# A stage of eight experts: dense tiles of tokens, and most tiles turned by DMA instead of by TensorE

## What is computed

```python
g = flat @ shared_gate.T
u = flat @ shared_up.T
shared_out = jax.nn.sigmoid(g) * u @ shared_down.T
weights = jax.nn.softmax(flat @ router_w.T, axis=-1)
top_w, top_idx = jax.lax.top_k(weights, TOPK)
comb = jnp.zeros_like(weights).at[jnp.arange(N)[:, None], top_idx].add(top_w)
ge = jnp.einsum('nh,eih->nei', xb, wg)
ue = jnp.einsum('nh,eih->nei', xb, wu)
he = jax.nn.sigmoid(ge) * ue
de = jnp.einsum('nei,ehi->neh', he, wd)
routed = (comb.astype(jnp.bfloat16)[:, :, None] * de).astype(jnp.float32).sum(axis=1)
return x + shared_out + routed
```

## Time and profile before

| what | value |
|---|---|
| time, median of 3 executions | 659.87 us (655.4 to 660.19) |
| the profiled execution | 653.7 us, of which its span is 651.7 us |
| granted TensorE clock over the span | 0.995 |
| busy share of the span | PE 93%, DVE 78%, ACT 72%, POOL 55% |
| busy tenths per fortieth of the span, from 80% to 95% of it (most of the expert stage) | PE 9, DVE 4 or 5, ACT 5 to 7 |

### The profile page before, as it was taken

One profiled execution on the slowest core, in us unless ns is written; L12 is line 12 of the kernel. 1 busy time (PEld: TensorE's weight loads), 2 busy tenths in 40 slices (PEclk: granted clock), 3 DMA queues, 4 the chain that ended last, 5 costly groups with the idle time before them and its releaser, 6 DMA issues.

```text
span 651.7 us, 12576 instructions
## 1 busy us (share of the span) xinstructions
PE 606.6 (93%) x4110; PEld 259.2 (40%) x4110; DVE 507.6 (78%) x970; ACT 472.0 (72%) x662; POOL 360.0 (55%) x494
## 2 busy tenths in 40 slices
PE   4799999999999999999999999879999999999987
PEld 4543333333333333333333332224554466666532
DVE  2479899999999999999999999964528654454577
ACT  3654899899899899899898888985432276667511
POOL 5559453684684684684684462251553577777310
PEclk9899999999999999999999999999999999999999
DMA  8642434534525535534433432115698533333178
GB/s 293 195 135 76 114 93 145 168 110 144 170 87 168 167 89 171 167 112 146 135 111 102 132 111 80 50 52 121 170 220 184 110 105 106 100 106 107 50 230 310
DMA packets 64990, 88.66 MB, mean 136 GB/s; under 512 B 12624, under 2 KB 45264, under 8 KB 63904
## 3 DMA queue, kind: packets, MB, share of 16 engines
q1 hardware_dynamic: 60032, 68.72, 34.4%
q0 software_dynamic: 4896, 19.14, 12.1%
HBM read 63.75 MB, written 32.74 MB: 148 GB/s over the span
## 4 chain that ended last, share of the span: by engine, by line
PE 76%; DVE 11%; issue 6%; ACT 5%; DMA 1%; POOL 1%; SPq 0%; ACTq 0%; DVEq 0%; POOLq 0%
PE PS L1083 17%; PE PS L986 11%; PE PS L1311 9%; PE PS L1055 8%; PE PS L1774 7%; DVE MX L996 7%; PE PS L845 5%; PE PS L1837 4%; PE PS L1585 4%; ACT E L1069 2%; PE PS L840 2%; PE PS L991 1%; PE PS L933 1%; PE PS L1732 1%; PE PS L929 1%
## 5 line engine op out<-in xcount | busy, mean ns | idle before, releaser
L996 DVE TENSOR_REDUCE MX<-PS 128x1 f32<-128x512 f32 x512 | 323.1, 683 | 17.3 <-PE PS L986 15.4
L1069 ACT ACTIVATE E<-PS 128x1024 f32<-128x1024 f32 x256 | 253.5, 1020 | 32.7 <-PE PS L1055 28.6
L986 PE MATMUL PS<-BIG 53*128 53x512 f16 x512 | 128.6, 384 | 12.2 <-DVE MX L996 10.8
L1083 PE MATMUL PS<-E,BIG 128*32 128x512 f32 x1024 | 136.4, 605 | 2.0 <-ACT E L1069 2.0
L1055 PE MATMUL PS<-BIG 55*128 55x512 f16 x512 | 101.2, 381 | 8.2 <-ACT E L1069 3.5
L879 POOL TENSOR_TENSOR ML<-BIG,ML 128x512 f32<-128x512 f32 x30 | 38.3, 1277 | 102.8 <-ACT BIG L855 102.6
L986 PEld LDWEIGHTS PS<-BIG 53*128 53x128 f16 x512 | 34.3, 93 | 134.0 <-DVE MX L996 120.1
L1796 DVE SCALAR_TENSOR_TENSOR E<-WP,PS 128x352 bf16<-128x352 f32 x39 | 20.3, 521 | 47.0 <-ACT WP L1786 47.0
L1774 PE MATMUL PS<-BIG,CT 128*128 x312 | 53.0, 313 | 1.8 <-DVE WP L1346 1.0
L855 ACT ACTIVATE BIG<-PS,BIG 128x256 f32<-128x256 f32 x64 | 35.7, 560 | 25.9 <-PE PS L840 14.5
L1856 POOL DMA_INDIRECT scr_ys<-SW,bvB x39 | 38.3, 981 | 20.8 <-DVE SW L1849 12.5
(11 more groups left out here) (261 smaller groups left out, 904.0 us busy)
## 6 DMA issues: line engine op xcount, KB each, us to landing
scr_parts<-WP SPq DMA_DIRECT2D x96, 128.0 KB
BIG<-scr_parts SPq DMA_DIRECT2D x64, 192.0 KB
BIG<-in_we POOLq DMA_DIRECT2D x8, 1088.0 KB, 14.1
scr_u<-ML SPq DMA_DIRECT2D x32, 256.0 KB, 3.0
X<-in_x SPq DMA_DIRECT2D x8, 512.0 KB, 6.5
CT<-in_ctx SPq DMA_DIRECT2D x8, 512.0 KB, 4.1
ML<-scr_u SPq DMA_DIRECT2D x16, 256.0 KB
ML<-scr_recs SPq DMA_DIRECT2D x16, 256.0 KB
```

The source lines that it names most:

```text
L986: e.matmul(PS[:, yi[name] % 3, :], QK[rows, qb(u), 0, j0 + jj, 128 * tt:128 * tt + 128], QK[rows, qb(u), 1, j0 + jj, :], start=True, stop= ...
L996: e.tensor_reduce(MX[:, g % 2, c:c + 1], PS[:, yi[name] % 3, :], AX.X, ALU.max)\
L1069: e.activation(E[:, st, 2 * jj:2 * jj + 2, :], PS[:, slot(name):slot(name) + 2, :], ACT.Exp, scale=1 / 1024).then_inc(s["rc"], 1)
L1083: ins = e.matmul(PS[32 * hh:32 * hh + 32, AVB, :], VT[:, b % 2, st, 4 * (g % 4) + hh, :], E[:, st, hh, :], start=(st == 0), stop=(st == 3))
```

## The change

The list of slots has no gaps any more: 4096 slots make 32 full tiles (`NS`), and an expert's border may fall inside a tile. What is looped over is 39 pieces, each a tile and an expert; a tile with a border in it is computed once for each expert in it. DVE works out for every piece its expert and its tile (`owners`, `pieces`) and a mask column of 0 or 0.5 for each of its 128 slots (`segments`, `masks`). `YS` is now a ring of 16 tiles; each is cleared first (`clear`), and `evac` adds the masked result of a piece to its tile, whose address comes from a register. Tile t is scattered once piece t + 7 is done. There are 32 gathers and 32 scatters where there were 39 of each.

The gathered tiles of the first two pairs are turned by PE as before; the other 28 tiles are turned by DMAs that SP issues, from `XS` to `XT`, which becomes a ring of ten tiles. Both operands of the gate and up matmuls now have an address from a register, so 16 registers are loaded every fourth pair.

```diff
+BY_PE = 2
...
-        late = E[:, 3, :, :].rearrange("p k t -> p (k t)").bitcast(BF)
-        XS += [late[:, 1024 * i:1024 * i + 1024].rearrange("p (a n) -> p a n", a=2) for i in range(4)]
-        XT = [cf[:, 2048 + 1024 * i:3072 + 1024 * i].rearrange("p (k n) -> p k n", k=4) for i in range(2)]
-        YS = [free[:, 1024 * i:1024 * i + 1024].rearrange("p (a n) -> p a n", a=2) for i in range(4)]
+        late_rows = ML[:, 0, :, :].rearrange("p a t -> p (a t)").bitcast(BF)
+        XS = [v[:, 1024 * i:1024 * i + 1024].rearrange("p (a n) -> p a n", a=2)
+              for v, n in ((cf, 2), (xf, 2), (late_rows, 4)) for i in range(n)]
+        XT = swh[:, 0:5120].bitcast(BF)
+        YS = E[:, 2:4, :, :].rearrange("p b k t -> p (b k t)").bitcast(BF)
...
-            dve.at(when(("G", 2, 1)) + .78 * dt_, weights)
+            dve.at(tb + 2., weights)
...
-                st(e, e.tensor_scalar(NI, PS[:, bank, 128:136], 127.0, None, ALU.add))
-                st(e, e.tensor_scalar(NI, NI, 7, None, ALU.logical_shift_right))
-                st(e, e.tensor_copy(TC, NI))
+                st(e, e.tensor_copy(TC, PS[:, bank, 128:136]))
...
+                inc, running = runs
+                st(e, e.tensor_copy(NI, BX))
+                st(e, e.tensor_scalar(NI, NI, 7, None, ALU.logical_shift_right))
+                st(e, e.tensor_copy(FE, NI))
+                st(e, e.scalar_tensor_tensor(ME, FE, -128.0, BX, ALU.mult, ALU.add))
+                st(e, e.tensor_scalar(ME, ME, 0.5, None, ALU.is_gt))
+                st(e, e.scalar_tensor_tensor(XE, TC, 0.5, ME, ALU.is_gt, ALU.mult))
+                st(e, e.tensor_tensor(XI, running(XE, J0, J1, 8), XE, ALU.subtract))
+                st(e, e.tensor_tensor(XI, XI, ME, ALU.add))
+                st(e, e.tensor_tensor(SE, FE, XI, ALU.add))
+                st(e, e.tensor_tensor(CM, bc(iotaf[:, :], NTILE), wide(SE), ALU.is_ge))
+                st(e, e.tensor_reduce(EF, CM, AX.X, ALU.add))
+            dve.at(when(("G", 2, 1)) + .77 * dt_, owners)
+
+            def pieces(e):
+                st = dch.step
+                st(e, e.tensor_tensor(C2, CM, wide(XI), ALU.mult))
+                st(e, e.tensor_reduce(XL, C2, AX.X, ALU.max))
+                st(e, e.tensor_scalar(EOF[:, :, 0], EF, -1.0, 4352.0, ALU.add, ALU.mult))
+                st(e, e.tensor_tensor(TU, iotaf[:, :], XL, ALU.subtract))
+                st(e, e.tensor_scalar(TT, TU, NS - 1.0, None, ALU.min))
+                st(e, e.tensor_scalar(MA, TT, 9.5, -10.0, ALU.is_gt, ALU.mult))
+                st(e, e.tensor_tensor(MC, TT, MA, ALU.add))
+                st(e, e.tensor_scalar(MA, TT, 19.5, -10.0, ALU.is_gt, ALU.mult))
+                st(e, e.tensor_tensor(MC, MC, MA, ALU.add))
+                st(e, e.tensor_scalar(MA, TT, 29.5, -10.0, ALU.is_gt, ALU.mult))
+                st(e, e.tensor_tensor(MC, MC, MA, ALU.add))
+                e.tensor_scalar(EOF[:, :, 1], MC, 512.0, None, ALU.mult).then_inc(s["rt"], 1)
+            dve.at(when(("G", 3, 0)) + .725 * dt_, pieces)
+
+            def segments(e):
+                st = dch.step
                 inc = runs[0]
-                dch.step(e, e.tensor_tensor(CM, bc(iotaf[:, :], NTILE),
-                                            inc.rearrange("p (o a) -> p o a", o=1).broadcast_to([128, NTILE, 8]),
-                                            ALU.is_ge))
-                dch.step(e, e.tensor_reduce(EF, CM, AX.X, ALU.add))
-                e.tensor_scalar(ET[:, :], EF, 7.0, 4352.0, ALU.min, ALU.mult).then_inc(s["rt"], 1)
-            dve.at(when(("G", 2, 1)) + .77 * dt_, owners)
+                st(e, e.tensor_tensor(C2, CM, wide(BX), ALU.mult))
+                st(e, e.tensor_reduce(LO, C2, AX.X, ALU.max))
+                st(e, e.tensor_tensor(C2, CM, wide(inc), ALU.mult))
+                st(e, e.tensor_reduce(HI, C2, AX.X, ALU.max))
+            dve.at(when(("G", 3, 0)) + .73 * dt_, segments)
+
+            def masks(e):
+                st = dch.step
+                st(e, e.scalar_tensor_tensor(LO, TU, -128.0, LO, ALU.mult, ALU.add))
+                st(e, e.scalar_tensor_tensor(HI, TU, -128.0, HI, ALU.mult, ALU.add))
+                st(e, e.tensor_scalar(LO, LO, PCOL, 0.5, ALU.is_lt, ALU.mult))
+                st(e, e.scalar_tensor_tensor(MKI, HI, PCOL, LO, ALU.is_ge, ALU.mult))
+                st(e, e.tensor_scalar(MA, TT, 15.5, -16.0, ALU.is_gt, ALU.mult))
+                st(e, e.tensor_tensor(MC, TT, MA, ALU.add))
+                e.tensor_scalar(ETO, MC, 512.0, None, ALU.mult).then_inc(s["mk"], 1)
+            dve.at(tb + .38, masks)
...
-            dve.at(when(item) + .12 * dt_, places)
+                e.scalar_tensor_tensor(OX[:, :], IA, -1.0, IN, ALU.add, ALU.add).then_inc(s["ox"], 1)
+            dve.at(tb + 1.9, places)
...
-                if j == 4:
-                    e.wait_ge(s["gu"], len(gi))
                 if j >= 8:
-                    e.wait_ge(s["xt"], j - 7)
-                for a in range(min(2, NTILE - 2 * j)):
...
+        def turned(t):
+            return 16 * (t // 8 + (t % 8 >= 2 * BY_PE) + 1)
+
+        def turn_by_dma(j, a):
+            t = 2 * j + a
+
+            def f(e):
+                e.wait_ge(s_xs[j % 8], 32 * (j // 8) + 32 - (0 if j % 8 else 16))
+                if j == BY_PE:
+                    e.wait_ge(s["gu"], len(gi))
+                if t >= 10:
+                    e.wait_ge(s["g2"], t - 2)
+                e.dma_start_transpose(XT[:, 512 * (t % 10):512 * (t % 10) + 512].rearrange("p (k n) -> p k n", k=4), XS[j % 8][:, a, :])\
+                    .then_inc(s_xt[t % 8], 16)
+            sp.at(tb + j - 2.7 + .2 * a if j > BY_PE + 1 else tb + t / 100, f)
...
         def turn_slots(j):
+            if j >= BY_PE:
+                for a in range(2):
+                    turn_by_dma(j, a)
+                return
...
-                if j >= 2:
-                    e.wait_ge(s["g2"], 2 * (j - 1))
-                e.activation(XT[j % 2], rows, ACT.Copy).then_inc(s["xte"], 1)
+                e.activation(XT[:, o:o + 1024], bank, ACT.Copy).then_inc(s["xte"], 1)
...
+                if 2 * BY_PE <= q < NS:
+                    e.wait_ge(s_xt[q % 8], turned(q))
                 if a == 0:
-                    if j:
+                    if 0 < j < BY_PE:
                         e.wait_ge(s["xte"], j + 1)
                     if j and j % 4 == 0:
                         n = min(8, NTILE - q)
-                        e.reg_load(regs[0:n], ET[0:1, q:q + n])
-                expert[q] = e.snap(regs[q % 8], min_val=0, max_val=7 * 4352)
+                        e.reg_load(regs[0:2 * n], ET[0:1, 2 * q:2 * q + 2 * n])
+                expert[q] = e.snap(regs[2 * (q % 8)], min_val=0, max_val=7 * 4352)
+                tile = e.snap(regs[2 * (q % 8) + 1], min_val=0, max_val=9 * 512)
                 for c in range(2):
                     for k in range(4):
-                        ins = e.matmul(PS[:, 2 * a + c, 0:352], XT[j % 2][:, k, 128 * a:128 * a + 128],
+                        ins = e.matmul(PS[:, 2 * a + c, 0:352], XT[:, bass.ds(tile + 128 * k, 128)],
...
+                    e.wait_ge(s["mk"], 1)
+                    held.extend(e.alloc_register(f"place{i}") for i in range(8))
+                if r % 8 == 0:
+                    n = min(8, NTILE - r)
+                    e.reg_load(held[0:n], ETO[0:1, r:r + n])
+                place = e.snap(held[r % 8], min_val=0, max_val=15 * 512)
+                if r:
+                    e.wait_ge(s["de2"], r)
+                if r < NS:
+                    e.wait_ge(s["zr"], r + 1)
+                e.wait_ge(s["d2"], r + 1)
+                e.scalar_tensor_tensor(YS[:, bass.ds(place, 512)], PS[:, 4 + a, :], MKI[:, r:r + 1], YS[:, bass.ds(place, 512)],
+                                       ALU.mult, ALU.add).then_inc(s["de2"], 1)
...
-                if j >= 4 and a == 0:
-                    e.wait_ge(s_ys[j % 4], 32 * (j // 4))
-                e.tensor_scalar(YS[j % 4][:, a, :], PS[:, 4 + a, :], 0.5, None, ALU.mult).then_inc(s["de2"], 1)
+                if r >= 16:
+                    e.wait_ge(s_ys[(r - 16) // 4], 64)
+                e.memset(YS[:, 512 * (r % 16):512 * (r % 16) + 512], 0.0).then_inc(s["zr"], 1)
+            if r < NS:
+                dve.at(tb + j + 1 + (.36 if a == 0 else .8), clear)
...
-                if r == 0:
+                t = r - 7
+                if t == 0:
                     e.wait_ge(s["ox"], 1)
                 e.wait_ge(s["de2"], r + 1)
-                e.indirect_dma_start(ys, bass.IndirectOffsetOnAxis(ap=OX[:, r:r + 1], axis=0), YS[j % 4][:, a, :], None)\
-                    .then_inc(s_ys[j % 4], 16)
+                e.indirect_dma_start(ys, bass.IndirectOffsetOnAxis(ap=OX[:, t:t + 1], axis=0),
+                                     YS[:, 512 * (t % 16):512 * (t % 16) + 512], None).then_inc(s_ys[t // 4 % 4], 16)
+            if r < 7:
+                return
...
```

(11 more changed lines are left out.)

81 lines of the change are left out of this document (47 added, 34 removed), and 2 rows, old and new, of the table s.

## The result

The changed kernel is slower: 661.76 us (median of 18 runs, 659.43 to 665.59) against 656.09 for the kernel before (18 runs, 652.52 to 660.19), a ratio of 1.0084 with a 95% interval of 1.006 to 1.0108, or 5.5 us more. The forecast was 657.3 from a base of 659.87, 2.6 us less. In all runs of this study, a few executions that took 697 to 1105 us enter neither a median nor a ratio.

What follows compares the result with a forecast made beforehand. PE was taken to bound the expert stage; the terms -7.9 + 3.3 + 2.0 = -2.6 us gave 657.3 us against the median of 659.87. The range was 650.5 to 672.

Steps and rivals of the forecast that it cites:

- What PE gets rid of: Expert stage: 18 of twenty blocks of eight transposes leave PE, taking 7.9 us off the time.
- Ahead of the stage: Before the expert stage, new index arithmetic on DVE delays its last shared product and so the first tanh: 3.3 us lost.
- PE's loads: Expert stage: four loads of 16 registers, 1.2 us each, 0.5 of it seen, cost 2.0 us; bounds nothing to 5.8.
- DVE is hidden: Expert stage: DVE's work with the added memset and addition takes 1.7 us a piece, under PE's 2.02, costing nothing.
- Turning DMAs: Expert stage: each tile's DMA takes 3 to 4 us, under the lead of 4.86 us, costing nothing.
- The hidden head: Ahead of the expert stage, DVE's new steps fit its idle time but for 1.0 us, loads covered: 653.0; chance 0.25.
- Late tiles: Expert stage: turning DMAs of 6.2 us exceed PE's lead and lose 9.8 us: 667; chance 0.17.
- one at a time: Expert stage: turning DMAs run singly, each for its whole latency; at 4.85 us each 79 us more: 736; chance 0.04.
- DVE as the bound: Expert stage: 32 memsets stretched to 1.0 us make DVE need 2.43 a piece, 13 us more: 670; chance 0.08.
- The sequencer: Gate and up matmuls: a second register address adds 7.2 us of PE sequencer time, all seen: 664.5; chance 0.08.

Runs made afterwards that it cites:

- e18: Kernel before with only the turning changed: from the third pair on, tiles are turned by DMA; 646.89 us against 657.91 for the kernel before, ratio 0.9833.
- e4: Changed kernel with the head reordered: `pieces` moved earlier, `segments` behind the first gathered hidden product; 660.02 us, ratio 1.006 to the kernel before.
- e3: Changed kernel with 36 more transposes on PE between the first pair's turn and the register load; 659.48 us, ratio 1.0048 to the kernel before.
- e2: Changed kernel with the gathered tile's address a constant, so PE loads 8 registers at a time, not 16; 657.17 us, ratio 1.0021 to the kernel before.
- e1: Changed kernel with a constant place for DVE's eviction, so DVE loads no registers; 656.38 us, ratio 1.0012 to the kernel before.
- e17: Changed kernel with split loads: PE 4 registers ahead of every pair, DVE 1 ahead of every eviction; 654.02 us against 657.91 for the kernel before, ratio 0.9941.

## Why the prediction was wrong

**What PE gets rid of, -7.9: right.** A pair without disturbance takes 4.02 us after (4.04 said), no gate and up waits for a DMA, and e18 alone brings 8.1.

**Ahead of the stage, +3.3: right in size, not in its reason.** The last shared product came where the working put it (524.7 and the offset of 1.7 make 526.4; it was 526.49). But it does not set the stage's start: the first gate and up was at 526.45 since PE's load of registers started at 524.57, behind `pieces`, and took 1.58 us, which the prediction had called covered at 523.6. The loss to that place is 2.6 us. ACT's copy of the first turned tile, the next thing that it waits for, ended at 523.56. In e4, which moves `pieces` forward, that copy is what comes last, and so e4 gains 1.6 and not more. Missed was what the idle time does next: the clock fell to half for 3.4 us and cost 1.6 in the first two pieces. That `masks` is hidden was right only because of that clock: where the clock holds, the third distance is 2.61 us (e3) and 2.73 (e2) in place of 2.01.

**PE's loads, +2.0: the right mechanism, too small.** A load of 16 registers was put at 1.2 us and was 1.39; seen of it were 0.9 to 1.2 us each and not 0.5, 3.8 in all, of which before had 1.4. With the head's share, halving them gives 4 us (e2), within the bound of 5.8.

**DVE is hidden, cost nothing: this is the step that failed.** Its working counts memset 0.25 (0.272), eviction 0.7 (0.751), hidden tile 0.52 and comes to 1.7 us a piece under 2.02, and all three hold. The diff also gives DVE `reg_load` of eight registers ahead of every eighth eviction, and the prediction gave it no price: "0.2 us of waits and registers". It is 2.0 us, five times, in a queue with 0.3 to 0.5 us to spare, and PE waits for what stands behind it: 5.7 us in the pieces beside the loads, of which 5.4 are gone in e1, whose time is 5 us less. Without it the changed kernel is level with the one before. It also shows what the test of a mean against 2.02 misses: one step of 2 us in eight pieces is a mean of 0.25, and hidden by that test.
The Trainium skill (Runtime: NRT & Kernel Launch, Instruction fetch mechanics) puts a TENSOR_LOAD at about 200 ns a register, for the runtime's own loads from HBM; these here are from SBUF. DVE comes near: 0.31 us for one and 2.0 for eight are 0.24 a register. PE does not: 0.33, 0.72 to 0.76 and 1.39 us for 4, 8 and 16 are 0.09 a register. The row of PE alone would have given DVE 0.7 us, too little to be seen as the cause.

**Turning DMAs, cost nothing: right.** They landed after 2.4 us (2.3 to 4.4), under the lead of 4.86; the value taken was 3 to 4. In e1 to e4 and e17 the medians are 2.7 to 3.2 and one DMA, in e3, took 5.3, which no engine waited for.
The Trainium skill's 1309 ns for 128x128 (VectorE: DVE Perf Modes, The three transpose paths), taken four times, would be an estimate of 5.2 us for a tile; the whole tile landed in 2.4, and SP's issue of it was 1.19.

**Rivals.** The hidden head: no. Late tiles and one at a time: no, by the landing times. DVE as the bound: the right engine by a wrong mechanism, since its memsets all took 0.272 us beside POOL's transfers, and the price of 13 us never came. The sequencer: its arithmetic grew from 46 ns to 74 to 83 with two addresses, and cost nothing (e2); its loads did cost, which came under the forecast's own term.

**The sum.** -7.9 + 2.6 + 1.6 (clock) + 5.7 (DVE's loads) + 2.4 (PE's, net) + 1.6 (shared blocks) = 6.0, against 6.2 in the traces and 5.5 in the times. Of the 8.6 us between this and the forecast of -2.6, DVE's loads are 5.7, the clock 1.6, the shared blocks 1.6 and PE's loads 0.4, less 0.7 that the head cost less than said; clock and shared blocks stood in no term of the forecast either. The result lies in the range given, and in absolute time near the forecast only because the three runs of before had a median 3.8 us above that of eighteen.

## What to carry to other kernels

When a diff gives an engine a `reg_load`, price it on that engine by the number of registers, and set its length against the slack of one turn of the loop, not against the mean. Load few registers often rather than many at once where the queue is close to its limit. Time two halves of a change apart before keeping both: here the turns by DMA are worth 11 us (e18), and the dense tiles cost some 16, if the difference of the two ratios, taken on two chips, is all theirs.
